# Attention's output is normalised and split inside attention; the routings are written out with four buffers of x; the output bias comes from TensorE

## The reference

```python
x = x + 0.5 * ffn(layernorm(x))          # 32 experts, top-1, capacity 1.25
x = x + attn(layernorm(x))               # 16 heads of 32
x = x + 0.5 * ffn(layernorm(x))

def attn(x):                             # q, k get rotary positions
    scores = einsum('bqhd,bkhd->bhqk', q, k) / sqrt(hd)
    out = einsum('bqhk,bkhd->bqhd', softmax(scores), v)
    return out @ Wo.T + bo

def ffn(xt):                             # T = 8192 tokens
    probs = softmax(xt @ w_router); top1 = argmax(probs)
    pos = cumsum(onehot(top1))[top1] - 1 # place in the expert's buffer
    # tokens with pos < C are gathered by expert, silu(g)*u, down, scattered back times the gate
```

## Time and profile before

| stage | from, us | length | PE | DVE | POOL | ACT | PEclk | DMA share |
|---|---|---|---|---|---|---|---|---|
| r1 | 0 | 246 | 176 | 165 | 66 | 126 | 1.00 | 0.45 |
| e1 | 246 | 759 | 733 | 529 | 289 | 280 | 1.00 | 0.52 |
| qkv | 1005 | 596 | 570 | 392 | 331 | 129 | 0.98 | 0.58 |
| attention | 1601 | 1863.5 | 1834 | 1374 | 1513 | 1262 | 0.98 | 0.33 |
| r2 | 3464.5 | 447.5 | 311 | 359 | 210 | 159 | 0.81 | 0.56 |
| e2 | 3912 | 759 | 734 | 529 | 294 | 280 | 0.98 | 0.52 |

### The profile page before, as it was taken

The page is one execution under the profiler, slowest core; times in us unless marked ns, Lnnn a source line. Parts: engine busy times, 40 slices in busy tenths (PEclk is TensorE's granted clock), DMA queues, the critical chain, the costliest instruction groups (busy, mean ns, idle before and its releaser), DMA issues. The chain is left out here.

```text
span 4671.3 us, 74949 instructions
## 1 busy us (share of the span) xinstructions
PE 4357.5 (93%) x26432; PEld 3134.4 (67%) x26432; DVE 3348.6 (72%) x6032; ACT 2235.8 (48%) x3619; POOL 2703.4 (58%) x1530
## 2 busy tenths in 40 slices
PE   6879999989999799999999999999958776999999
PEld 6769998978888555555555555555526666998898
DVE  6767777766666577777777777777738886777776
ACT  4533333322222166766666667666643433333333
POOL 2333333425555468888888888888865553333343
PEclk9999999989999899999999999999988887999999
DMA  4455555535555613333333333333335554555553
GB/s 136 147 201 186 180 180 180 184 135 179 178 180 176 173 44 80 77 73 74 74 73 73 79 80 77 73 74 74 73 86 170 155 162 157 183 180 181 180 184 125
DMA packets 429557, 616.41 MB, mean 132 GB/s; under 512 B 187452, under 2 KB 188752, under 8 KB 429248
## 3 DMA queue, kind: packets, MB, share of 16 engines
q1 hardware_dynamic: 398528, 545.72, 41.0%
q0 software_dynamic: 30720, 66.62, 3.8%
HBM read 451.98 MB, written 177.80 MB: 135 GB/s over the span
## 5 line engine op out<-in xcount | busy, mean ns | idle before, releaser
L1646 DVE TENSOR_REDUCE att_halves<-att_mx 128x1 f32<-128x512 f32 x2048 | 1274.6, 684 | 444.7 <-PE att_mx L1694 442.7
L1562 POOL TENSOR_TENSOR att_pairsum<-att_p,att_p 128x1024 f32<-128x1024 f32 x512 | 1207.7, 2380 | 344.8 <-ACT att_p L1589 344.7
L1589 ACT ACTIVATE att_p<-att_st 128x512 f32<-128x512 f32 x2048 | 1122.4, 597 | 343.5 <-PE att_st L1714 330.1
L1714 PE MATMUL att_st<-att_q,att_k 128*128 128x512 f32 x2048 | 870.6, 427 | 8.8 <-ACT att_p L1589 3.8
L1694 PE MATMUL att_mx<-att_k,att_q 96*128 96x512 f32 x2048 | 822.1, 406 | 23.1 <-DMA att_v<-v 22.4
L1714 PEld LDWEIGHTS att_st<-att_q,att_k 128*128 128x128 f32 x2048 | 386.8, 189 | 535.9 <-issue 245.0
L1724 PE MATMUL att_op<-att_p,att_v 128*32 128x512 f32 x4096 | 541.8, 601 | 0.7 <-ACT att_p L1589 0.7
L893 DVE TENSOR_TENSOR e_w<-e_raw,e_w 128x2048 fp32r<-128x2048 f32 x192 | 439.0, 2287 | 43.1 <-ACT e_w L888 43.1
L1694 PEld LDWEIGHTS att_mx<-att_k,att_q 96*128 96x128 f32 x2048 | 394.4, 193 | 108.3 <-issue 23.2
L912 ACT ACTIVATE e_sg<-e_gp 128x320 f32<-128x320 f32 x256 | 112.1, 438 | 731.7 <-PE e_up L182 731.7
L888 ACT ACTIVATE e_w<-e_raw 128x2048 fp32r<-128x2048 f32 x192 | 367.1, 1912 | 43.7 <-DMA e_raw<-in_w_gate 38.7
(11 more groups left out here) (154 smaller groups left out, 8663.0 us busy)
## 6 DMA issues: line engine op xcount, KB each, us to landing
e_raw<-in_w_gate SPq DMA_DIRECT2D x64, 1024.0 KB, 8.6
e_raw<-in_w_up SPq DMA_DIRECT2D x64, 1024.0 KB, 11.0
e_raw<-in_w_down SPq DMA_DIRECT2D x64, 1024.0 KB
att_q<-q SPq DMA_DIRECT2D x192, 256.0 KB, 4.2
att_k<-k SPq DMA_DIRECT2D x192, 256.0 KB, 6.3
r_x<-in_x SPq DMA_DIRECT2D x16, 1024.0 KB, 6.1
x<-r_base SPq DMA_DIRECT2D x16, 1024.0 KB, 9.9
qkv_x<-x SPq DMA_DIRECT2D x16, 1024.0 KB, 8.6
```

The lines of the kernel that those rows point to most:

```text
L1562: nc.gpsimd.tensor_tensor(out=pairsum[h][PLACE[g]][:, :], in0=pr[h][2 * g % RING][:, :], in1=pr[h][(2 * g + 1) % RING][:, :], op=ALU.add). ...
L1589: nc.scalar.activation(pr[h][kt % RING][:, half(c)], st[(4 * kt + x) % NB][:, :], ACT.Exp, scale=SCALE).then_inc(s_exp, 1)
L1646: nc.vector.tensor_reduce(out=halves[:, h, qt, c:c + 1], in_=mx[n % NB][:, :], axis=AX.X, op=ALU.max).then_inc(s_max, 1)
L1714: nc.tensor.matmul(st[(4 * kt + x) % NB][:, :], kst[b][:, h, kt * P:(kt + 1) * P], qst[b][:, h, c * HALF:(c + 1) * HALF], start=True, stop ...
```

## The change

It does four things.

1. **In attention**, the output of each pair is normalised and split before it is stored. SP stores the pair's sums, reads them back as 128 x 16 (`zt`), DVE inverts them (`invert`), SP stores the inverses and reads them back spread over each head's rows (`zi`, four transfers); POOL multiplies (`scale`), ACT makes the high part (`hi_o`), POOL the low part (`rest`), and SP stores both (eight transfers). All this runs one step later than the store did: pair p-2 in step p.
2. **In r2**, what attention now does is gone: the inversion, the loads of `inverse`, `divide`, `hi_ao`, `lo_ao`. SP loads the two parts straight into the product's operands `ao`, in three buffers.
3. **The bias** of the output projection is no longer added by DVE: each tile's accumulation on PE begins with one product of `both` (ones in two rows, zero elsewhere) by `bo_sb` (the bias's high part in one row, its low part in the other).
4. **Both routings** are written out without hardware loops, x has four buffers, and the first loads stand in another order: x ahead of most constants, and in r2 the weights and `ao` first of all.

```diff
@@ route, buffers and loads
+    NX = 4
+    NA = 3
-        x = S.pair(sb, "x", [P, TJ, D])
+        x = [sb(f"x{b}", [P, TJ, D]) for b in range(NX)]
@@ route, SP
+            def load(r):
+                sp.wait_ge(s_xn, past(TJ * (r - NX + 1)))
+                sp.wait_ge(s_base, past(TJ * (r - NX + 1)))
+                sp.dma_start(x[r % NX][:, :, :], x_ap(x_in, r)).then_inc(s_x[r % NX], 16)
+            def load_ao(r):
+                sp.wait_ge(s_op, past(TJ * (r - NA + 1)))
+                for part in range(2):
+                    sp.dma_start(ao[r % NA][part][:, :, :].bitcast(F32), ao_ap(part, r)).then_inc(s_ao[r % NA], 16)
...
+            for r in range(NG):
+                store_base(r)
+                if attn and r + NA < NG:
+                    load_ao(r + NA)
+                if r + NX < NG:
+                    load(r + NX)
@@ route, GpSimd
-            def divide(i, par):
-                pool.wait_ge(s_ao_in[par], 16 * (1 + P // HD) * (i + 1))
-                nc.gpsimd.tensor_tensor(out=aof[par][:, :, :], in0=aof[par][:, :, :], in1=inv[par][:, :, :],
-                                        op=ALU.mult).then_inc(s_ao, 1)
-            def lo_ao(i, par):
-                pool.wait_ge(s_ao_hi, 2 * i + par + 1)
-                nc.gpsimd.tensor_tensor(out=ao[par][1][:, :, :], in0=aof[par][:, :, :],
-                                        in1=ao[par][0][:, :, :].bitcast(F32), op=ALU.subtract).then_inc(s_ao_lo, 1)
@@ route, VectorE
-                nc.vector.reciprocal(sums[:, :], sums[:, :]).then_inc(s_inv, 1)
-            def bias(i, par):
-                dve.wait_ge(s_x[par], 16 * (i + 1))
-                nc.vector.tensor_tensor(out=x[par][:, :, :], in0=x[par][:, :, :],
-                                        in1=bo_sb[:, :].unsqueeze(1).broadcast_to([P, TJ, D]),
-                                        op=ALU.add).then_inc(s_xb, 1)
@@ route, TensorE
+                nc.tensor.matmul(op[j][:, :], both[:, :], bo_sb[:, :], start=True, stop=False)
@@ attention, SP
+            def give_sums(p):
+                sp.wait_ge(s_zo, p + 1)
+...
+                sp.wait_ge(s_z_stored, 16 * 4 * (p + 1))
+                sp.dma_start(zt[p % 2][:, :], pair_rows(sums, p).rearrange(
+                    "h (b t) -> (h b) t", t=ZT)).then_inc(s_zt, 16)
+            def take_inverse(p):
+                sp.wait_ge(s_inv, p + 1)
+                sp.dma_start(pair_rows(inverse, p).rearrange("h (b t) -> (h b) t", t=ZT),
+                             zt[p % 2][:, :]).then_inc(s_inv_stored, 16)
+                sp.wait_ge(s_inv_stored, 16 * (p + 1))
+                sp.wait_ge(s_on, past(p - 1))
+...
             def step(i, b, left):
+                p = DEPTH * i + b
                 if left >= 2:
                     load(*ahead(i, b, 2))
-                if i + b > 0:
-                    store(DEPTH * i + b - 1, (b + 1) % 2)
+                if p > 1:
+                    take_inverse(p - 2)
+                if p > 0:
+                    give_sums(p - 1)
+                if p > 1:
+                    store(p - 2)
@@ attention, GpSimd
             def step(i, b, left):
                 for g in range(NG2):
                     for h in range(2):
                         add(p, g, h)
+                    if g == 0 and p > 1:
+                        scale(p - 2)
                     if g == 1:
                         for h in range(2):
                             join(p, h)
+                        if p > 1:
+                            rest(p - 2)
@@ attention, ScalarE
+                        if p > 1 and (kt, x) == (4, 3):
+                            hi_o(p - 2)
@@ attention, VectorE
+                for qt in range(FIRST, KT):
+                    if left:
+                        maxima(*ahead(i, b, 1), qt)
+                    if qt == FIRST and p > 1:
+                        invert(p - 2)
```

More of the change, by code:

```diff
@@ L242, in route @@
         s_unset = sem("s_unset")
-        s_x = S.pair(sem, "s_x")
+        s_x = [sem(f"s_xin{b}") for b in range(NX)]
         s_stats = sem("s_stats")
@@ L353, in _ @@
[L353 to L366 removed]
+            for r in range(2, NX):
+                if attn and r < NA:
+                    load_ao(r)
+                load(r)
@@ new lines, in _ @@
+            norm(0)
+            norm(1)
+            copies(0, range(TJ))
+            bases(0, range(TJ))
+            for r in range(NG):
+                exps(r)
+                if r + 1 < NG:
+                    copies(r + 1, (0, 1))
+                    bases(r + 1, (0, 1))
+                if r + 2 < NG and not attn:
+                    norm(r + 2)
+                if r + 1 < NG:
+                    copies(r + 1, (2, 3))
+                    bases(r + 1, (2, 3))
+                if r + 2 < NG and attn:
+                    norm(r + 2)
@@ L1415, in _, with attention @@
             rounds_ahead(pe, NG, step)
-def attention(nc, name, q_in, k_in, v_in, cst, ao_out, sum_out):
+def attention(nc, name, q_in, k_in, v_in, cst, ao_out, sums, inverse):
     S = Space(nc, name)
@@ L1680, in _ @@
             rounds_out(DEPTH, NP, step)
+            for p in (NP - 2, NP - 1):
+                invert(p)
         @block.tensor
```

441 lines of the change are left out of this document (194 added, 247 removed).

## The result

The changed kernel takes 4628.43 us, median of four runs (4627.49 to 4632.08); the kernel before 4674.94 in the same sessions (the fourth run brought its median from 4674.76 to that). The ratio is 0.9905, 95% interval 0.9888 to 0.9922: 1% faster, some 46 us. The forecast was 4598. The profiled execution took 4632.08 us, its span is 4629.0.

What follows compares the result with a forecast made beforehand. PE bounds e1, e2, qkv and attention, DVE bounds r2, with PE close behind in r1. 4671.3 - 122.6 (r2) - 13.0 (r1) + 17.8 + 41 (attention) = 4594.5, plus 2.0 and 1.4: 4598 us, range 4548 to 4650.

Steps and rivals of the forecast that it cites:

- The loop in attention: Attention, SP's queue: load, inverse, spread loads, `scale` to `rest`, stores' issue, load again; 29.1 us against 28.34, 41 us lost.
- load 9.7: Attention's loop: from the load's first issue to its landing, seven issues 2.7 and landing 7.0 later.
- spread loads 3.3: Attention's loop: the inverses' spread loads take 3.3 us after the inverse has landed.
- inverse landed 0.3: Attention's loop: the small store of the inverse lands 0.3 us after the load, since transfers land in issue order.
- a loop of 29.7 to 30.5: Attention: rival case of a longer loop, total up to 4665 us; chance 0.06.
- The chain at attention's end: Attention's end: sums stored to last stores landed, 20.9 us where it took 3.1; 17.8 lost.
- a sign of being wrong: Attention: the prediction is wrong if, among other signs, POOL's sums come late for `totals`.
- the stalls of DVE: r2: `r_run` (3.69 us) and `r_ok` (3.95) stand still while POOL runs wide instructions; 3.5 and 3.8 a round go.
- The credit for the bias: r2: DVE loses the bias instruction, 2.29 with a gap of 0.1, 2.4 us a round.
- register instructions of the loops and the waits on `met` cost at most a tenth a round; I count nothing: r1: writing out the hardware loops was credited with no gain.
- `choose` can begin at 127.5 instead of 128.26: r1: with four buffers DVE then waits for the logits; 0.75 us a round saved, 14 times, 10.5.
- the range: Whole kernel: 4548 to 4650 us, leaving out some 0.2 of the chance.

Runs made afterwards that it cites:

- a_load_early: Changed kernel with the load of pair p+3 issued ahead of the store of pair p-2 on SP's queue in attention; 4540.88 us, ratio 0.9717.
- experiment 9: Changed kernel with two 128 x 2048 multiplications a group put back on GpSimd in r2, on a buffer nobody reads; 4723.79 us, ratio 1.0098.
- experiment 8: Changed kernel with the output bias added by DVE again, once a group, and no bias product on PE; 4629.71 us, ratio 0.9900.
- experiment 4: Changed kernel with the inverse of pair p-2 stored and spread ahead of the load of pair p+2 on SP's queue; 5021.31 us, ratio 1.0746.

## Why the prediction was right or wrong

**The loop in attention: right in place, wrong in size.** The prediction named the loop, said PE would run seven pairs unharmed and then wait at the first rough product, and put the period at 29.1 us. PE ran six, its first wait stands at 1803.46, and the period is 29.87. Its terms, as means over 50 turns of the changed kernel's trace, beside the forecast: load's first issue to inverse landed 10.57 (9.7 + 0.3), spread loads and the step to `scale` 3.60 (3.3), `scale` to `rest` 11.90 (12.1), the stores' issue 3.81 (3.7). So the terms that were mis-sized are "load 9.7", which is 10.38 to its last landing (the last of the seven issues stands 3.14 behind the first, forecast 2.7, and lands in 7.24, forecast 7.0), and "spread loads 3.3", by 0.3; "inverse landed 0.3" is 0.19. A part of it is issues that take long: 24 of 984 on SP's queue in these turns take over 0.8 us, up to 2.1, instead of 0.43. The error is 0.77 us in 29.1, under 3%. But what is lost is the difference of the period to 28.3, and that doubled: 55 pairs at 1.55 is 85 us where 41 was forecast. This, 44 us, is the largest miss, larger than that of the total. The case "a loop of 29.7 to 30.5" had been given 0.06.

**The chain at attention's end.** Forecast 17.8 lost. From PE's last matmul to the next stage's first transfer there were 3.8 us before (3460.8 to 3464.6) and 21.0 in a_load_early (3434.5 to 3455.5): 17.2 lost. (The terms that the prediction lists add up to 20.5, not to its 20.9; from the issue of the last sums to the next stage it is 20.4 in the changed kernel, 3525.56 to 3545.95.) What the prediction had at nothing is POOL's two more instructions in the last two steps, where PE has fewer rough products to do or none. ACT's copies of the last three sums stood 24.7 and 19.4 us apart before, and stand 24.8 and 26.2 apart now: 6.9 us lost. From 3469.0 to 3524.1 POOL runs without a pause, and PE waits 7.4 us for its sums (3.2 before), which the prediction had named as a sign of being wrong. In a_load_early, where POOL has fallen less behind, it is 3.2 us. The loop's 85, the end's 17 and these 7 make up attention's 110.6 but for some 1.

**r2.** The rounds are 17.76 us, forecast 17.7, with PE as the bound and no wait for rows. In all 121.4 saved, forecast 122.6: 98.7 between PE's first product and its last (100.2), 22.2 by the earlier start (20.4; it came out at 15.3 us into the stage, forecast 17), 0.5 at the end (2). That the stalls of DVE were GpSimd's doing was read from two pairs of ends, and experiment 9 shows it: two wide instructions a group cost 93 us. The credit for the bias, 2.4 us a round on DVE, was worth nothing in time (experiment 8), since PE bounds the round.

**r1: the way right, the size wrong.** Forecast 13.0 saved, measured 30.9. Two steps failed. First, "register instructions of the loops and the waits on `met` cost at most a tenth a round; I count nothing": with two buffers and the old order, the code written out has rounds of 13.1 for 13.8, and the rounds together are 8.1 us shorter. Second, "`choose` can begin at 127.5 instead of 128.26": this took PE's end as fixed. But PE's `positions` waits for DVE's `r_onehot`, and DVE's `choose` for PE's products. The round is that chain: `r_onehot` 111.70, `positions` 112.10, products until 121.72, `choose` 121.76, `r_onehot` 123.55. Its part on PE was 10.6 us before (116.80 to 127.39) and is 9.6 now, since PE no longer waits in it for ACT's turned rows, and all of it is done at the lower clock. The start of r1 came out right: the first `r_onehot` is 3.4 us earlier, forecast 2.5. Holding one side still, the prediction saw 12.9 for 11.85.

**The sum.** 17.9 us more gained in r1, 51.8 more lost in attention and 0.6 elsewhere make the span 34.5 us longer than the 4594.5 forecast. 3.1 us lie around the span (forecast 2.0), and the median lies 3.7 below the profiled execution, where the forecast had it 1.4 above: 4628 for 4598. That 4628 lies well inside the range is in part luck: r1's extra gain, from steps that the prediction had wrong, hides a third of what attention lost beyond the forecast. The chance that the change is faster was well placed: r2 alone gave 121 us, and by the prediction's own sum the loop could take that only from 30.5 us on.

## What to carry to other kernels

When an issue on an in-order queue is put behind a result, walk the queue round once: from its transfer through every wait back to itself. If the sum is near the loop's own period, a 3% error in it decides the gain, so give the queue's order slack (here the load ahead of the store) instead of computing whether it just fits. A small transfer whose landing is waited for doesn't belong behind a large one, on the same queue or another. And where two engines wait for each other in turn, cost the round as one chain, never one engine with the other's times held fixed. An engine that does its work in order and has one instruction of such a chain among it (here ACT's `hi_o`) hands the chain's delay on to all that stands behind that instruction.

## What the runs showed of the hardware that was not expected

- A transfer of 8 KB on ACT's queue landed only behind the 256 KB transfers in flight on SP's: 3.0 us median against 1.4 alone.
- With two buffers, a 1 MB store issued 0.5 us ahead of a load delays the load by 2 us (8.0 instead of 6.0 from issue to landing) and the round by 2.4.
- Code written out instead of a hardware loop was worth 0.5 to 0.7 us in a round of 13.8 on engines that wait for each other.
- The granted clock's column reads 1.00 for r1, where the trace has no record of it, while PE's turns take 1.09 us as at a granted clock of 0.50 and not the 0.60 of 1.00.
- After a wait of 6.2 us PE took 4.91 us, at a granted clock of 0.50, for what it does in 2.85 otherwise (experiment 4).
